# GpSimd's splits and sums in instructions of 256 columns, in a graph network with attention on one core

## The chip, the cores and the metric

The kernel runs on one core of a Trainium2 chip, in one launch. The metric is device time: the median of three runs of the kernel before is 2378.5 us (2378.1 to 2378.63). Five engines work at once and meet only at semaphores: TensorE (PE) multiplies and writes PSUM, VectorE (DVE), ScalarE (ACT) and GpSimd (POOL) do element-wise work, SyncE (SP) issues most DMAs.

## The reference

1024 nodes of 512 features in 16 graphs, 16,384 edges. All arrays are fp32.

```
h = relu(layernorm(x));  h = gcn_in(batchnorm(h))
for i in 4 layers:
    h = h + attention(ln(h), cond[16, 256, 512], Wq, Wk, Wv, Wo)   # 8 heads of 64
    u = ln(h) @ geglu_w[i] + geglu_b[i];  val, gate = split(u)      # 512 -> 4096
    h = h + (val * gelu(gate)) @ ffo_w[i] + ffo_b[i]                # 2048 -> 512
out = x + (gcn_out(h) + relu(layernorm(x)))
```

`gcn` multiplies by a weight matrix and sums over the edges with the usual degree scaling.

## The kernel before, in words

**Splits.** Every fp32 operand of a matrix product is kept as a high part (fp32r) and a low part, the rest. A product is three matmuls: high by high, high by low, low by high (lines 2367 to 2369, 2616 to 2619, 2741 to 2745). ACT writes the high parts by a copy. GpSimd or VectorE writes the low parts by a subtraction, `low = whole - high`, a TENSOR_TENSOR with two inputs in SBUF.

**Products of 2 by 2 blocks.** Keys, values and the wide MLP matrix are computed with seven block products in place of eight. That needs sums of weight blocks (`sums_s`, written by VectorE at L2250 to L2255 in the MLP and L1693 to L1698 in attention), sums of condition blocks (`cond_sum`, GpSimd, L798) and sums of activation blocks (`t_sums`, VectorE, L2227), whose low parts come from L2232 and L2237.

**Stages.** First the edges are counted and the first convolution is done (to about 180 us). Then come four layers. A layer's attention goes over 8 pairs of graphs (`value_units(t)` and `key_units(t)`, t = 0 to 7). In layer 0 only, GpSimd also makes the split blocks `cb` of the next pair's condition there, 7 low parts (`cond_low`, L803) and 4 sums a pair, and SP saves them to DRAM; later layers load them back. A layer's MLP goes over q = 0 to 7. For q = 1 to 7 there are two weight sets c = 0, 1 (`set_low(q, c)`, buffer `wg_lo`); `down_low(q)` splits the down projection (`wf_lo`), `f_low` (L864, 512 columns) the activations. The set (1, 0) is multiplied as a full block set, all others by the seven products.

**What sets the order.** Each engine runs one fixed list of instructions. Each `wait_ge` waits for a semaphore. `w_ok` counts finished low weight pieces: PE waits for it before it uses a piece (`full_product`, `set_product`, L2741), and SP before it loads the next piece into one of the two `stage` slots. `c_lo` and `c_sum` count low condition blocks and condition sums. At the start of an MLP GpSimd does, one behind the other, `down_low(0)` (L732), `set_low(1, 0)` (L890, L894), three `f_low` (L864), `set_low(1, 1)` (L890, L897). Beside it VectorE does the sums and low parts of the activations (L2227, L2232). `rsqrt` and `first_rsqrt` (L727, L773) are small powers by GpSimd, on which the layer norms wait.

Of the kernel before, what the change touches and what calls it, by code (L numbers as in the profile page):

```python
# [5 lines left out]
def gnn_preln_kernel(  # L6
# [24 lines left out]
    ALU = mybir.AluOpType  # L31
# [71 lines left out]
    with ExitStack() as ctx:  # L103
        def sb(name, shape, dt, where=ctx):
            return where.enter_context(nc.sbuf_tensor(name, shape, dt))

        def sem(name):
            return ctx.enter_context(nc.semaphore(name))


        stage = sb("stage", [P, 2, 1024], f32)
# [242 lines left out]
        c_hi, c_lo, c_sum = sem("c_hi"), sem("c_lo"), sem("c_sum")  # L354
# [8 lines left out]
        w_hi_ok, w_ok = sem("w_hi_ok"), sem("w_ok")  # L363
# [28 lines left out]
        def wait_apart(eng, on, value):  # L392


            eng.wait_ge(on, value)
            eng.sem_inc(waited, 1)

        def bits(ap):

            return ap.bitcast(f32)  # L400
# [24 lines left out]
        def attn_place(part, kind, k):  # L425
            return ((wk_hi, wk_lo), (wv_hi, wv_lo))[kind][part][:, k]
# [8 lines left out]
        def attn_piece(kind, k, l):  # L435

            if l == 0:
                return 2 + 2 * kind + k
            return FIRST_PIECES + PIECES * (l - 1) + (KEY_PIECE, VALUE_PIECE)[kind][k]
# [7 lines left out]
        def raw_block(g, n):  # L447

            row, col = {11: (0, 0), 12: (0, 1), 21: (1, 0), 22: (1, 1)}[n]
            return (stage if g else raw0)[:, row, :].rearrange("p (k b m) -> p b k m", k=2, b=2)[:, col]  # L450

        def cond_source(g, j):
            return (raw_block(g, 11), t2_s[:, :, :], t1_s[:, :, :], raw_block(g, 21), raw_block(g, 22),
                    raw_block(g, 12), raw_block(g, 11))[j]
# [30 lines left out]
        def set_piece(q, c):  # L485
            return DOWN_PIECE[q - 1] + 1 + c

        def set_place(part, c):
            return (wg_hi, wg_lo)[part][:, 1 - c].rearrange("p k v n -> p (k v n)")[:, 0:7 * 256]\
                .rearrange("p (b n) -> p b n", n=256)  # L490
# [7 lines left out]
        def short_set(l, q, c):  # L498
            return (SETS - 1) * l + 2 * (q - 1) + c - 1
# [197 lines left out]
        def _(pool):  # L697
# [31 lines left out]
            def w_low(n, slot, hi, lo):  # L729

                pool.wait_ge(w_hi_ok, n + 1)
                pool.tensor_tensor(lo, stage[:, slot, :], bits(hi), ALU.subtract).then_inc(w_ok, 1)  # L732


            pool.wait_ge(d5_ok, 1)
# [9 lines left out]
            for half in range(2):  # L745
# [8 lines left out]
                pool.tensor_scalar(x_nm[:, part], x_nm[:, part], -1.0, None, ALU.mult).then_inc(x_rs, 1)  # L754
            d_low_of(1)
            w_low(0, 0, gcn_place(0, 0), gcn_place(1, 0))
            pool.wait_ge(b_ln, 2 * KC)
            pool.tensor_scalar(x_veps[:, 0:KC], x_mv[:, 0:KC, 1], EPS, None, ALU.add).then_inc(b_rs, 1)
# [16 lines left out]
            def attn_low(kind, k, l):  # L775

                n = attn_piece(kind, k, l)
                hi, lo = attn_place(0, kind, k), attn_place(1, kind, k)
                pool.wait_ge(w_hi_ok, n + 1)
                pool.tensor_tensor(lo[:, 0:3, :], stage[:, n % 2, 256:1024].rearrange("p (b n) -> p b n", n=256),  # L780
                                   bits(hi[:, 0:3, :]), ALU.subtract)
                pool.tensor_tensor(lo[:, 3:7, :], sums_s[:, :, :], bits(hi[:, 3:7, :]), ALU.subtract)\
                    .then_inc(w_ok, 1)

            def cond_sum(g, n):

                out, a, b = ((t1_s[:, :, :], raw_block(g, 12), raw_block(g, 11)),
                             (t2_s[:, :, :], raw_block(g, 22), t1_s[:, :, :]),
                             (raw_block(g, 12), raw_block(g, 22), raw_block(g, 12)),
                             (raw_block(g, 11), raw_block(g, 21), t2_s[:, :, :]))[n]  # L790
                if n == 0:
                    wait_apart(pool, raw_in, 16 * g + 16)
                elif n == 1 or n == 2:
                    pool.wait_ge(c_sum, 4 * g + 1)
                else:
                    pool.wait_ge(c_sum, 4 * g + 2)
                    pool.wait_ge(c_lo, BLOCKS * g + 1)
                pool.tensor_tensor(out, a, b, ALU.subtract).then_inc(c_sum, 1)  # L798

            def cond_low(g, j):  # L800

                pool.wait_ge(c_hi, BLOCKS * g + j + 1)
                pool.tensor_tensor(cb[:, j, 1], cond_source(g, j), bits(cb[:, j, 0]), ALU.subtract).then_inc(c_lo, 1)  # L803

            def wq_low(l, half):

# [34 lines left out]
            first_sums()  # L841
            pool.wait_ge(a_low, NT + 1)
            attn_low(KEYS, 0, 0)
            for n in range(3):
                cond_sum(0, n)
            attn_low(KEYS, 1, 0)
            for half in range(2):
                wq_low(0, half)
            cond_low(0, 0)
            cond_sum(0, 3)  # L850
            cond_low(0, 1)
            first_rsqrt(0)
            pool.wait_ge(z2_ok, FIRST)
            for j in range(2, 5):
                cond_low(0, j)
# [3 lines left out]
            for l in range(L):  # L859
# [8 lines left out]
                def down_low(q):  # L868
                    r = DOWN_PIECE[q]
                    w_low(FIRST_PIECES + PIECES * l + r, r % 2, down_place(0, q), down_place(1, q))  # L870

                def ahead_low(q):
                    if l < L - 1:
                        attn_low(KEYS, q, l + 1)
                    else:
                        r = KEY_PIECE[q]
                        w_low(FIRST_PIECES + PIECES * l + r, r % 2, gcn_place(0, q), gcn_place(1, q))
# [4 lines left out]
                def set_low(q, c):  # L882
                    r = set_piece(q, c)
                    hi, lo = set_place(0, c), set_place(1, c)
                    full_set = (q, c) == (1, 0)
                    if not full_set:

                        pool.wait_ge(s_ok, 4 * (short_set(l, q, c) + 1))
                    pool.wait_ge(a_hi_ok, SETS * l + 2 * (q - 1) + c + 1)
                    pool.tensor_tensor(lo[:, 0:3, :], stage[:, r % 2, 256:1024].rearrange("p (b n) -> p b n", n=256),  # L890
                                       bits(hi[:, 0:3, :]), ALU.subtract)
                    pool.wait_ge(w_hi_ok, FIRST_PIECES + PIECES * l + r + 1)
                    if full_set:
                        pool.tensor_tensor(lo[:, A21, :], stage[:, r % 2, 0:256], bits(hi[:, A21, :]),  # L894
                                           ALU.subtract).then_inc(w_ok, 1)
                    else:
                        pool.tensor_tensor(lo[:, 3:7, :], sums_s[:, :, :], bits(hi[:, 3:7, :]),  # L897
                                           ALU.subtract).then_inc(w_ok, 1)

                first_rsqrt(2 * l + 1)  # L900
# [10 lines left out]
                if l == 0:  # L911
                    for n in range(3):
                        cond_sum(1, n)
# [46 lines left out]
                wait_apart(pool, x3_ok, 2 + NT * l + NT)  # L960
                down_low(0)
                set_low(1, 0)
                f_low(0, 0, 0, 0)
                f_low(0, 1, 0, 1)
                f_low(0, 2, 1, 0)
                set_low(1, 1)
                f_low(0, 3, 1, 1)
                for q in range(1, MG):
                    if q > 1:
                        down_low(q)  # L970
                    f_low(q, 0, 1, 0)
                    f_low(q, 1, 0, 0)
                    if q == 1:
                        down_low(q)
                    if q + 1 < MG:
                        set_low(q + 1, 0)
                    f_low(q, 2, 1, 1)
                    f_low(q, 3, 0, 1)
                    if q + 1 < MG:
                        set_low(q + 1, 1)  # L980
                    if q in KEYS_IN:
                        ahead_low(KEYS_IN.index(q))
# [2064 lines left out]
```

## Time and profile before

| | |
|---|---|
| median of three runs | 2378.5 us |
| the profiled execution | 2377.68 us |
| its span | 2375.9 us |
| granted TensorE clock, mean | 0.996 |
| PE busy | 2315.6 us, 97% |
| VectorE busy | 1658.8 us, 70% |
| ScalarE busy | 1243.8 us, 52% |
| GpSimd busy | 1038.9 us, 44% |

PE, the bound, has 60.3 us without work in the span. Times of the rows are microseconds from the span's start. An idle time in brackets is what the engine waited before the row, with the instruction that ended it. An instruction's duration counts from its start to its end, and holds what it waited for a port.

### The profile page before, as it was taken

The page shows a single profiled execution, that of the slowest core. Times are in us where ns is not written, and L with a number is a line of the kernel's source. Part 1 is how long each engine was busy: PE and PEld are TensorE (multiplying, and loading weights), DVE is VectorE, ACT ScalarE, POOL GpSimd, SP SyncE. Part 2 cuts the span into 40 slices and gives each one's busy share as a digit, 9 for nine tenths or more (in the row PEclk, how much of TensorE's full clock was granted, in tenths as well). Part 3 has the DMA queues.
Part 4 walks back from the last instruction along what each step waited for, and adds up shares of the span by engine and source line. Part 5 has one row for each costly group of instructions (what it writes and reads, how often), then busy time and mean ns, then how long its engine had stood idle before and what let it go on. Part 6 is the DMA issues. An engine that isn't in the chain of part 4 may idle for free.

```text
span 2375.9 us, 38716 instructions
## 1 busy us (share of the span) xinstructions
PE 2315.6 (97%) x14414; PEld 2043.8 (86%) x14414; DVE 1658.8 (70%) x3053; ACT 1243.8 (52%) x2585; POOL 1038.9 (44%) x696
## 2 busy tenths in 40 slices
PE   7899999999999999999999999999999999999999
PEld 5358999988888999988888999988888999988887
DVE  9976776786657676786657666786667667785554
ACT  9955767654434555653434555644434655643322
POOL 3025877566653322266652322266652322265530
PEclk9999999999999999999999999999999999999999
DMA  2033333212232333212232333222232433122230
GB/s 80 1 132 135 146 148 152 98 49 67 62 120 79 118 106 106 82 54 62 63 120 80 123 107 106 74 60 61 61 117 81 125 116 108 63 63 62 62 125 36
DMA packets 115882, 214.57 MB, mean 90 GB/s; under 512 B 9520, under 2 KB 71600, under 8 KB 113904
## 3 DMA queue, kind: packets, MB, share of 16 engines
q1 hardware_dynamic: 115408, 207.89, 26.6%
q10 hardware_dynamic: 288, 4.19, 0.4%
q8 instruction: 117, 1.92, 0.3%
q14 instruction: 69, 0.57, 0.1%
HBM read 176.13 MB, written 35.91 MB: 89 GB/s over the span
## 4 chain that ended last, share of the span: by engine, by line
PE 84%; DVE 9%; POOL 2%; ACT 2%; issue 2%; DMA 0%; DVEq 0%; SPq 0%; ACTq 0%; POOLq 0%
PE ps L2367 9%; PE ps L2368 9%; PE ps L2369 9%; PE ps L2616 9%; PE ps L2619 8%; PE ps L2618 8%; PE ps L2741 7%; PE ps L2743 7%; PE ps L2745 7%; PE ps L2644 2%; PE ps L2666 2%; PE ps L2668 2%; DVE oh_d L1683 1%; PE ps L2943 1%; PE ps L2663 1%
## 5 line engine op out<-in xcount | busy, mean ns | idle before, releaser
L2616 PE MATMUL ps<-cb,wk_hi 128*128 128x256 f32 x896 | 258.3, 288 | 4.6 <-POOL cb L803 3.6
L2616 PE MATMUL ps<-wv_hi,cb 128*128 128x256 f32 x896 | 257.4, 287 | 4.6 <-DVE kv L1985 4.4
L2618 PE MATMUL ps<-cb,wk_hi 128*128 128x256 f32 x896 | 253.7, 283 | 0.0
L2619 PE MATMUL ps<-cb,wk_lo 128*128 128x256 f32 x896 | 253.7, 283 | 0.0
L2619 PE MATMUL ps<-wv_hi,cb 128*128 128x256 f32 x896 | 253.7, 283 | 0.0
L2618 PE MATMUL ps<-wv_lo,cb 128*128 128x256 f32 x896 | 253.7, 283 | 0.0
L864 POOL TENSOR_TENSOR f_lo<-ff,f_hi 128x512 fp32r<-128x512 f32 x128 | 168.7, 1329 | 172.0 <-ACT f_hi L1484 171.9
L823 POOL TENSOR_TENSOR v_lo<-kv,v_hi 128x512 fp32r<-128x512 f32 x96 | 124.4, 1296 | 260.2 <-ACT v_hi L1238 260.1
L2302 DVE TENSOR_TENSOR h<-h,ps 128x512 f32<-128x512 f32 x256 | 169.3, 684 | 65.4 <-PE ps L2369 64.8
L2368 PE MATMUL ps<-wf_lo,f_hi 128*128 128x512 f32 x512 | 199.3, 389 | 0.0
L2367 PE MATMUL ps<-wf_hi,f_hi 128*128 128x512 f32 x512 | 199.3, 389 | 0.0
L2369 PE MATMUL ps<-wf_hi,f_lo 128*128 128x512 f32 x512 | 199.3, 389 | 0.0
L2741 PE MATMUL ps<-xT_hi,wg_hi 128*128 128x512 f32 x480 | 187.8, 391 | 11.2 <-POOL wg_lo L897 6.8
L2743 PE MATMUL ps<-xT_lo,wg_hi 128*128 128x512 f32 x480 | 187.0, 390 | 0.0
L2745 PE MATMUL ps<-xT_hi,wg_lo 128*128 128x512 f32 x480 | 186.9, 389 | 0.0
L1985 DVE TENSOR_TENSOR kv<-ps,kv 128x512 f32<-128x512 f32 x192 | 132.3, 690 | 70.8 <-PE ps L2619 66.4
L2616 PEld LDWEIGHTS ps<-cb,wk_hi 128*128 128x128 f32 x896 | 171.7, 192 | 10.9 <-POOL cb L803 5.0
L2616 PEld LDWEIGHTS ps<-wv_hi,cb 128*128 128x128 f32 x896 | 171.7, 192 | 7.8 <-DVE kv L1985 5.8
L2618 PEld LDWEIGHTS ps<-cb,wk_hi 128*128 128x128 f32 x896 | 171.9, 192 | 1.1
L2618 PEld LDWEIGHTS ps<-wv_lo,cb 128*128 128x128 f32 x896 | 171.9, 192 | 0.0
L2619 PEld LDWEIGHTS ps<-wv_hi,cb 128*128 128x128 f32 x896 | 171.9, 192 | 0.0
L2619 PEld LDWEIGHTS ps<-cb,wk_lo 128*128 128x128 f32 x896 | 171.8, 192 | 0.0
(377 smaller groups left out, 6892.0 us busy)
## 6 DMA issues: line engine op xcount, KB each, us to landing
cb<-cb_s SPq DMA_DIRECT2D x168, 512.0 KB, 4.6
stage<-in_pieces SPq DMA_DIRECT2D x256, 128.0 KB, 2.6
cb_s<-cb SPq DMA_DIRECT2D x56, 512.0 KB, 2.6
stage<-in_pieces SPq DMA_DIRECT2D x44, 512.0 KB, 3.7
stage<-in_condT SPq DMA_DIRECT2D x7, 1024.0 KB, 5.8
stage<-in_pieces SPq DMA_DIRECT2D x16, 256.0 KB, 3.3
at_s<-at_hi ACTq DMA_DIRECT2D x2, 2048.0 KB, 11.8
wo_raw<-in_pieces SPq DMA_DIRECT2D x8, 512.0 KB, 4.4
```

Of the source, the lines that this page charges most:

```text
L864: pool.tensor_tensor(f_lo[q % 2][:, c, half * HALF:(half + 1) * HALF], ff[:, s % 2, :], bits(f_hi[q % 2][:, c, half * HALF:(half + 1) * HA ...
L1985: dve.tensor_tensor(wide(kv_temp(which)), ps[:, bank, :], wide(other[:, :, :]), ALU.add)\
L2302: dve.tensor_tensor(h[:, t, :], h[:, t, :], ps[:, down_bank(q, t), :], ALU.add)\
L2367: pe.matmul(bank, l_hi, r_hi, start=(first and i == 0), stop=False)
L2368: pe.matmul(bank, l_hi, r_lo, start=False, stop=False)
L2369: end = pe.matmul(bank, l_lo, r_hi, start=False, stop=(last and i == n - 1))
L2616: pe.matmul(to, l_hi, r_hi, start=(fresh and i == 0 and k == 0), stop=False, skip_group_check=True)
L2618: pe.matmul(to, l_hi, r_lo, start=False, stop=False, skip_group_check=True)
L2619: last = pe.matmul(to, l_lo, r_hi, start=False, stop=(k == 1), skip_group_check=True)
L2741: pe.matmul(ps[:, bank, :], hi[:, a, r], moving[0][:, n, :], start=(first and n == 0), stop=False, skip_group_check=True)
L2743: pe.matmul(ps[:, bank, :], hi[:, a, r], moving[1][:, n, :], start=False, stop=False, skip_group_check=True)
L2745: last = pe.matmul(ps[:, bank, :], lo[:, a, r], moving[0][:, n, :], start=False, stop=(n == 1), skip_group_check=True)
```

## The change

Four places of GpSimd's program are cut into instructions of 256 columns: `w_low` (1024 columns), `attn_low` (768 and 1024), `cond_sum` and `cond_low` (512), and `set_low` (768 and 1024). The semaphore is raised by the last piece alone. `f_low`, `kv_low`, `wq_low` and `wo_low` stay as they are, and so do all other engines.

```diff
             def w_low(n, slot, hi, lo):
                 pool.wait_ge(w_hi_ok, n + 1)
-                pool.tensor_tensor(lo, stage[:, slot, :], bits(hi), ALU.subtract).then_inc(w_ok, 1)
+                for c in range(0, 768, 256):
+                    pool.tensor_tensor(lo[:, c:c + 256], stage[:, slot, c:c + 256], bits(hi[:, c:c + 256]), ALU.subtract)
+                pool.tensor_tensor(lo[:, 768:1024], stage[:, slot, 768:1024], bits(hi[:, 768:1024]), ALU.subtract)\
+                    .then_inc(w_ok, 1)
...
             # attn_low; set_low has the same two loops
-                pool.tensor_tensor(lo[:, 0:3, :], stage[:, n % 2, 256:1024].rearrange("p (b n) -> p b n", n=256),
-                                   bits(hi[:, 0:3, :]), ALU.subtract)
-                pool.tensor_tensor(lo[:, 3:7, :], sums_s[:, :, :], bits(hi[:, 3:7, :]), ALU.subtract)\
-                    .then_inc(w_ok, 1)
+                for b in range(3):
+                    pool.tensor_tensor(lo[:, b, :], stage[:, n % 2, 256 * b + 256:256 * b + 512], bits(hi[:, b, :]),
+                                       ALU.subtract)
+                for b in range(3):
+                    pool.tensor_tensor(lo[:, 3 + b, :], sums_s[:, b, :], bits(hi[:, 3 + b, :]), ALU.subtract)
+                pool.tensor_tensor(lo[:, 6, :], sums_s[:, 3, :], bits(hi[:, 6, :]), ALU.subtract).then_inc(w_ok, 1)
...
             # cond_sum
-                pool.tensor_tensor(out, a, b, ALU.subtract).then_inc(c_sum, 1)
+                pool.tensor_tensor(out[:, 0], a[:, 0], b[:, 0], ALU.subtract)
+                pool.tensor_tensor(out[:, 1], a[:, 1], b[:, 1], ALU.subtract).then_inc(c_sum, 1)
             def cond_low(g, j):
                 pool.wait_ge(c_hi, BLOCKS * g + j + 1)
-                pool.tensor_tensor(cb[:, j, 1], cond_source(g, j), bits(cb[:, j, 0]), ALU.subtract).then_inc(c_lo, 1)
+                hi, lo, source = bits(cb[:, j, 0]), cb[:, j, 1], cond_source(g, j)
+                pool.tensor_tensor(lo[:, 0], source[:, 0], hi[:, 0], ALU.subtract)
+                pool.tensor_tensor(lo[:, 1], source[:, 1], hi[:, 1], ALU.subtract).then_inc(c_lo, 1)
```

GpSimd at the start of a layer's MLP, before (`wf_lo` and `wg_lo` are low weights, `f_lo` low activations):

```order
L732 TENSOR_TENSOR wf_lo<-stage,wf_hi 128x1024
L890 TENSOR_TENSOR wg_lo<-stage,wg_hi 128x768
L894 TENSOR_TENSOR wg_lo<-stage,wg_hi 128x256
L864 TENSOR_TENSOR f_lo<-ff,f_hi 128x512 x3
L890 TENSOR_TENSOR wg_lo<-stage,wg_hi 128x768
L897 TENSOR_TENSOR wg_lo<-sums_s,wg_hi 128x1024
L864 TENSOR_TENSOR f_lo<-ff,f_hi 128x512 x3
```

and in the changed kernel:

```order
L733 TENSOR_TENSOR wf_lo<-stage,wf_hi 128x256 x3
L734 TENSOR_TENSOR wf_lo<-stage,wf_hi 128x256
L899 TENSOR_TENSOR wg_lo<-stage,wg_hi 128x256 x3
L903 TENSOR_TENSOR wg_lo<-stage,wg_hi 128x256
L872 TENSOR_TENSOR f_lo<-ff,f_hi 128x512 x3
L899 TENSOR_TENSOR wg_lo<-stage,wg_hi 128x256 x3
L907 TENSOR_TENSOR wg_lo<-sums_s,wg_hi 128x256 x3
L908 TENSOR_TENSOR wg_lo<-sums_s,wg_hi 128x256
L872 TENSOR_TENSOR f_lo<-ff,f_hi 128x512 x3
```

Nothing changes places: ahead of the first `f_lo` there are eight instructions in place of three. VectorE's list beside it is the same in both kernels (`z` are the activations and their sums, `w_lo` here their low parts):

```order
L2232 TENSOR_TENSOR w_lo<-z,w_hi 128x3x2x128
L2227 TENSOR_TENSOR z<-z 128x3x256 x2
L2227 TENSOR_TENSOR z<-z 128x256 x4
L2232 TENSOR_TENSOR w_lo<-z,w_hi 128x3x2x128 x2
L2217 SCALAR_TENSOR_TENSOR ff<-ps,cols_sb,gel 128x512
L2250 TENSOR_TENSOR sums_s<-stage 128x256
```

All but the one with `ps` have two inputs in SBUF.

## Rows read from the trace of the kernel before

**Rows 1.** The page's first part: busy us (share of the span), instructions.

```profile
PE 2315.6 (97%) x14414; PEld 2043.8 (86%) x14414; DVE 1658.8 (70%) x3053; ACT 1243.8 (52%) x2585; POOL 1038.9 (44%) x696
```

**Rows 2.** PE's waits over the whole span: us in total, times, longest us.

```profile
PE ps L2741 <- POOL wg_lo L897: 6.8, 4, 1.7
PE ps L2741 <- POOL wg_lo L894: 4.4, 4, 1.1
PE ps L2616 <- POOL cb L803: 3.6, 7, 0.7
```

**Rows 3.** A group by form on GpSimd: busy us, mean ns, idle before.

```profile
L897 POOL TENSOR_TENSOR wg_lo<-sums_s,wg_hi 128x1024 fp32r<-128x1024 f32 x52 | 125.5, 2414 | 0.0
```

**Rows 4.** Timeline of GpSimd, 96 to 99 us: start us, us, instruction.

```profile
96.57 0.72 POOL L831 TENSOR_TENSOR sums_s<-stage 128x256 f32<-128x256 f32 x1 [58.06 <-DVE counts L1807]
97.26 0.72 POOL L832 TENSOR_TENSOR sums_s<-stage 128x256 f32<-128x256 f32 x1
```

**Rows 5.** Timeline of GpSimd, 166 to 181 us.

```profile
166.71 1.86 POOL L780 TENSOR_TENSOR wk_lo<-stage,wk_hi 128x768 fp32r<-128x768 f32 x1 [5.23 <-ACT wk_hi L1015]
168.52 2.39 POOL L782 TENSOR_TENSOR wk_lo<-sums_s,wk_hi 128x1024 fp32r<-128x1024 f32 x1
...
178.31 1.29 POOL L803 TENSOR_TENSOR cb<-t_s,cb 128x512 fp32r<-128x512 f32 x1
179.56 1.01 POOL L773 TENSOR_TENSOR x_veps<-x_veps,mhalf 128x4 f32<-128x4 f32 x1
```

**Rows 6.** Timeline of VectorE, 27 and 252 us.

```profile
27.50 0.16 DVE L1669 TENSOR_TENSOR bn<-x_veps,cols_sb 128x4 f32<-128x4 f32 x1 [0.69 <-POOL x_veps L760]
...
252.75 2.80 DVE L2018 TENSOR_TENSOR qbd<-z,qbd 64x256 fp32r<-64x256 f32 x2
```

**Rows 7.** Timeline of PE in layer 0, the instructions that waited.

```profile
182.58 0.33 PE L2684 MATMUL ps<-ident,o_full 128*128 128x128 f32 x1 [1.23 <-DVE p_exp L1937]
...
227.57 0.39 PE L2616 MATMUL ps<-wv_hi,cb 128*128 128x256 f32 x1 [1.07 <-DVE kv L1985]
...
238.99 0.38 PE L2616 MATMUL ps<-cb,wk_hi 128*128 128x256 f32 x1 [0.68 <-POOL cb L803]
...
258.78 0.39 PE L2616 MATMUL ps<-wv_hi,cb 128*128 128x256 f32 x1 [1.01 <-DVE kv L1985]
```

**Rows 8.** Timeline of ScalarE, 234 us.

```profile
234.75 0.60 ACT L1219 ACTIVATE kv<-ps 128x512 f32<-128x512 f32 x1 [2.54 <-POOL v_lo L823]
```

**Rows 9.** Timeline of GpSimd at the start of layer 0's MLP, and later in it.

```profile
488.63 2.99 POOL L732 TENSOR_TENSOR wf_lo<-stage,wf_hi 128x1024 fp32r<-128x1024 f32 x1 [5.03 <-DVE xT_lo L2091]
491.58 2.58 POOL L890 TENSOR_TENSOR wg_lo<-stage,wg_hi 128x768 fp32r<-128x768 f32 x1
494.12 1.43 POOL L894 TENSOR_TENSOR wg_lo<-stage,wg_hi 128x256 fp32r<-128x256 f32 x1
...
504.09 1.86 POOL L890 TENSOR_TENSOR wg_lo<-stage,wg_hi 128x768 fp32r<-128x768 f32 x1 [0.36 <-DVE sums_s L2255]
505.91 2.54 POOL L897 TENSOR_TENSOR wg_lo<-sums_s,wg_hi 128x1024 fp32r<-128x1024 f32 x1
...
608.45 2.41 POOL L897 TENSOR_TENSOR wg_lo<-sums_s,wg_hi 128x1024 fp32r<-128x1024 f32 x1
```

**Rows 10.** Timeline of VectorE there; the last row from a wide window merges six.

```profile
488.38 0.96 DVE L2232 TENSOR_TENSOR w_lo<-z,w_hi 128x768 fp32r<-128x768 f32 x1
489.26 3.18 DVE L2227 TENSOR_TENSOR z<-z 128x768 f32<-128x768 f32 x1
...
489.26 9.91 DVE L2227 TENSOR_TENSOR z<-z 128x768 f32<-128x768 f32 x6
```

**Rows 11.** Timeline of PE there, and at a later set (619 us).

```profile
495.61 0.50 PE L2741 MATMUL ps<-xT_hi,wg_hi 128*128 128x512 f32 x1 [1.10 <-POOL wg_lo L894]
508.51 0.50 PE L2741 MATMUL ps<-xT_hi,wg_hi 128*128 128x512 f32 x1 [1.72 <-POOL wg_lo L897]
...
619.15 0.39 PE L2741 MATMUL ps<-xT_hi,wg_hi 128*128 128x512 f32 x1
```

More of the change, by code:

```diff
@@ L889, in set_low @@
                     pool.wait_ge(a_hi_ok, SETS * l + 2 * (q - 1) + c + 1)
-                    pool.tensor_tensor(lo[:, 0:3, :], stage[:, r % 2, 256:1024].rearrange("p (b n) -> p b n", n=256),
-                                       bits(hi[:, 0:3, :]), ALU.subtract)
+                    for b in range(3):
+                        pool.tensor_tensor(lo[:, b, :], stage[:, r % 2, 256 * b + 256:256 * b + 512],
+                                           bits(hi[:, b, :]), ALU.subtract)
                     pool.wait_ge(w_hi_ok, FIRST_PIECES + PIECES * l + r + 1)
@@ L896, in set_low @@
                     else:
-                        pool.tensor_tensor(lo[:, 3:7, :], sums_s[:, :, :], bits(hi[:, 3:7, :]),
+                        for b in range(3):
+                            pool.tensor_tensor(lo[:, 3 + b, :], sums_s[:, b, :], bits(hi[:, 3 + b, :]), ALU.subtract)
+                        pool.tensor_tensor(lo[:, 6, :], sums_s[:, 3, :], bits(hi[:, 6, :]),
                                            ALU.subtract).then_inc(w_ok, 1)
```

## The prediction

> **What bounds the kernel now.** I read the page's busy shares first. PE works 2315.6 us of the 2375.9 us span [rows 1], so the time can move only by its 60.3 us of idle time, or by new idle time. Next come PE's waits. Few name GpSimd: 6.8 us for the last piece of the set (1, 1), 4.4 us for that of the set (1, 0), once each a layer, and 3.6 us for condition blocks in layer 0 [rows 2]. So GpSimd's 1038.9 us are mostly hidden, and the question is where its later end shows. I then read the timelines around each of these waits.
>
> **What one cut costs.** GpSimd's 256-column subtractions of the trace last 0.72 us and follow each other at 97.26 - 96.57 = 0.69 us [rows 4]. The 768-column one is followed after 168.52 - 166.71 = 1.81 us, the 512-column one after 179.56 - 178.31 = 1.25 us [rows 5], the 1024-column one lasts 2.39 to 2.41 us [rows 3, 5], a pitch of about 2.37. Cut up: 3 x 0.69 = 2.07, 2 x 0.69 = 1.38, 4 x 0.69 = 2.76. So one more instruction costs about 0.13 us: +0.26 for 768, +0.13 for 512, +0.39 for 1024 columns.
> By the code there are 43 `w_low` (3 more instructions each), 15 `attn_low` (5 more), 56 `set_low` (2 more) of which 52 have sums (3 more), 56 `cond_low` and 32 `cond_sum` (1 more): 129 + 75 + 268 + 88 = 560 more instructions, 560 x 0.13 = 73 us of GpSimd's time.
> The Trainium skill, GPSIMD Engine Reference, section Elementwise — side-by-side cycle accounting, gives 4497 ns for 2048 columns and 2.6 cycles a column at 1.2 GHz, which leaves an estimated 60 ns for what an instruction costs beside its columns. By that, 560 cuts would be 34 us; the rows of this trace say twice as much, and they decide.
>
> **What a cut changes for VectorE.** The timelines at 488 to 496 us show the two engines taking turns at one port. VectorE's L2227 of 768 columns lasts 3.18 us while GpSimd's L732 runs, and ends 0.8 us behind it; an uncontended one of that size lasts 0.96 us (the L2232 at 488.38) [rows 9, 10]. GpSimd's next, L890, lasts 2.58 us where 1.86 is normal, its L894 1.43 us where 0.72 is [rows 4, 9]. So each instruction with two SBUF inputs waits for one of the other engine: 0.72 us if VectorE's has 768 columns. From the ends of these rows, a turn takes 0.60 us for 256 columns on GpSimd, and 0.80 us (768) or 0.27 us (256) on VectorE. Pieces shorten VectorE's waits, and give it more turns between GpSimd's.
> The Trainium skill, SBUF — State Buffer, section Who interferes with whom, says that the second to issue waits until the first has finished. It does not say who is served next when GpSimd has more in its queue; on that see rival A.
>
> **Term 1, the MLP's start, four times.** Before, GpSimd did L732, L890 and L894 from 488.63 and PE began the full set at 495.61, after 1.10 us of idle time [rows 9, 11]. Now there are 4 + 3 + 1 = 8 pieces. VectorE has queued, in its order, the L2232 under way, L2227 with 768, 768, 256, 256, 256, 256 columns, and L2232 with 768. With one turn each, from 489.25 (when the L2232 leaves the port): 8 x 0.60 + 3 x 0.80 + 4 x 0.27 = 8.28, to 497.53; with 0.1 for the end, PE begins at 497.65, 2.04 us later.
> In return VectorE has its sums of activations 4 us sooner. But its next `ff` (L2217) waits for a `f_low` of GpSimd, which now comes later, and its weight sums take turns with two more `f_low`, about 1.17 us each (1.25 less the gap). By the same turns the last sum (L2255) ends at 503.2, where it ended at 504.02. GpSimd then has 3 + 4 pieces, 7 x 0.60 = 4.20, between which VectorE takes three turns of 256 columns and one of 1024 (0.27 x 3 + 1.07), then two gaps of 0.09: from 503.3 to about 509.55. PE needs 508.51 - 1.72 - 495.61 = 11.18 us for the full set, so is ready at 508.83, and starts the next set at 509.65 in place of 508.51. **+1.1 us a layer, +4.4 us**. Bounds: if the second set is in time, PE's own shift stays, 508.83 - 508.51 = +0.3; if VectorE takes more turns in the second stretch too, +2.0; and if the earlier sums win outright, -1.1 (rival C). What is queued behind the cut instructions on GpSimd (`f_low`) is needed by the down projection only after the next set.
>
> **Term 2, layer 0's first attention steps.** From 166.71 GpSimd works without a gap to 180.57; PE's transposes wait 1.23 us for a layer norm that waits for L773 [rows 5, 7]. Ahead of it now are one `attn_low` (+0.26 + 0.39) and three condition instructions (+0.39). **+1.0 us**; bounds 0.6 (if PE has slack that the rows do not show) and 1.3.
>
> **Term 3, the second pair's condition blocks.** The `attn_low` of the values (+0.65, of which the shorter turns of VectorE's `qbd` give back some) releases the load of the next condition, and two `cond_sum` (+0.26) the copy behind which the wait of 1.07 us at 227.57 stands: +0.85. Six more condition instructions stand ahead of ScalarE's copy at 234.75, which waited 2.54 us for GpSimd [rows 8], and one in PE's wait at 238.99 [rows 7]: together +0.65 + 9 x 0.12, +1.7. At 252.75 VectorE's two `qbd` take 2.80 us beside 512-column sums, where two turns of 0.6 and their own 0.85 make 1.85 [rows 6]: 0.95 back. With three more cuts ahead (+0.36) the wait at 258.78 ends +1.1 later than before, and that is what stays, since PE arrives there 1.7 - 1.01 = 0.7 later. **+1.1 us**; bounds 0.3 and 2.3.
>
> **Term 4, the other pairs.** Six times PE waits 0.49 us ((3.6 - 0.68) / 6) for a `cond_low` that starts after a small power [rows 2, 7]: 6 x 0.12, **+0.7 us**; bounds 0 and 1.
>
> **Term 5, the start.** `w_low(0)` stands ahead of the batch norm's power, and VectorE waits 0.69 us for it [rows 6]; VectorE sets the pace there. **+0.4 us**; bounds 0 and 0.5.
>
> **At nothing.** In the MLP's other sets GpSimd's last piece ended at 608.45 + 2.41 = 610.86, PE took up that set at 619.15 [rows 9, 11]: 8.3 us of cover for about 1.3 us of cuts a set and its neighbours. Without cover it would cost 0.65 us at each of 48 sets, 31 us. Loads that start later, by up to 2 us, are hidden the same way.
>
> **Sum.** 4.4 + 1.0 + 1.1 + 0.7 + 0.4 = 7.6 us. On the profiled execution, 2377.68 + 7.6 = 2385.3; that execution stands 0.8 us under the median, so the median is to be 2386.1: **2386 us**, slower by 0.32%.
>
> **Rivals.**
> A, GpSimd keeps the port through its own queue. Then the eight pieces run from 489.25 in 8 x 0.69 = 5.5 us, PE begins 0.7 us sooner, VectorE falls behind, and the second set ends at about 509.0: +0.5 a layer. 3.2 + 2.0 = 5.2, so 2383.7. Against it: between L732, L890 and L894, which stood ready in the queue, VectorE did get a turn each time [rows 9, 10].
> B, the cuts are hidden. If the pieces overlap so that 256 columns cost no more than a quarter of 1024 (0.59), terms 2 to 5 vanish and term 1 keeps some turns: 0 to +3 us, about 2379.5. For it: PE's idle time is only 2.5% [rows 1]. Against it: the pitch of 0.69 is measured on four such instructions [rows 4].
> C, the other side: VectorE's relief decides. Place: the second wait at the MLP's start, 1.72 us. If the weight sums end over 1.5 us sooner than in my turns (before 501.7), the second set is ready before PE is; if also the first wait grows only by 5 cuts, 0.65 us, a layer gains 1.72 - 0.65 = 1.07, 4.3 in all. It decides once terms 2 to 5 come to less than 4.3; at their lower bounds (0.9) the time is 2375.1. For it: VectorE's six L2227 take 9.91 us [rows 10], of which at 0.96 us for 768 and 0.42 us for 256 columns 2 x 0.96 + 4 x 0.42 = 3.6 us are work. Against it: the `ff` that waits for `f_low`.
> D, the turns hurt more: +2.0 in term 1 and the upper bounds elsewhere: 8.0 + 5.1 = 13.1, so 2391.6.
>
> **How the numbers follow.** My forecast (the sum within 2.5 us) 0.45, A 0.13, B 0.21, C 0.08, D 0.13. About 0.2%, 4.8 us, is what can be told from no change: the bound is 2383.3. My forecast and D lie above it but for 0.03 of the forecast, A by half: slower 0.62. Within it are 0.03 of the forecast, half of A, 0.20 of B and 0.03 of C, whose 2375.1 is itself too near: same 0.32. Faster by over 0.2% is the rest of C, where both waits go, and 0.01 of B: 0.06. The range leaves out C's lower end and D's upper: 2378 to 2391.
>
> **What would show it.** GpSimd's busy time 60 to 90 us higher, 1256 instructions. VectorE's six L2227 at the MLP's start within 6 to 7 us. PE's wait for the full set about 3.1 us, for the next about 0.8. PE's wait before the transposes 2.2 us, for condition blocks some 0.6 each. My account is wrong if the wait for the full set stays below 2 us, if PE waits for GpSimd at sets of q over 1, or if the time falls.

## The result and the profile after

The changed kernel takes 2387.8 us (median of 6 runs, 2387.1 to 2389.1), the kernel before, on the same chip, 2378.3 (2377.1 to 2378.6): 1.0042 times as long, 95% interval 1.0032 to 1.0053, so 9.5 us slower. The forecast was 2386, slower, in a range of 2378 to 2391. The profiled execution has a span of 2386.0 us, 10.1 more than before.

The first part of the page after (busy us, share of the span, instructions):

```profile
PE 2318.6 (97%) x14414; PEld 2048.2 (86%) x14414; DVE 1645.2 (69%) x3053; ACT 1244.8 (52%) x2585; POOL 1131.0 (47%) x1256
```

Against [rows 1], GpSimd is 92.1 us busier with 560 more instructions, 0.16 us each: by the rows 0.13 is the instruction's own, and the rest I put down to waits at the port. VectorE is 13.6 us less busy. Neither number is the loss; that stands in PE's waits (us in total, times, longest):

```profile
PE ps L2752 <- POOL wg_lo L903: 12.9, 4, 3.2
PE ps L2627 <- POOL cb L811: 6.1, 8, 1.3
PE ps L2752 <- POOL wg_lo L908: 1.1, 1, 1.1
```

They answer to [rows 2]: the wait for the full set rose from 4.4 to 12.9 us, that for the second set fell from 6.8 to 1.1, that for condition blocks rose from 3.6 to 6.1.

To see where the time went, I compared the moments at which PE goes on after its last wait ahead of each layer's MLP. Its timeline before, then after (start us, us, instruction, idle time before it):

```profile
488.50 0.38 PE L2367 MATMUL ps<-xT_hi,w_hi 128*128 128x256 f32 x1 [0.43 <-DVE xT_lo L2091]
...
1021.24 0.38 PE L2367 MATMUL ps<-xT_hi,w_hi 128*128 128x256 f32 x1 [0.43 <-DVE xT_lo L2091]
...
1553.77 0.38 PE L2367 MATMUL ps<-xT_hi,w_hi 128*128 128x256 f32 x1 [0.43 <-DVE xT_lo L2091]
...
2086.25 0.38 PE L2367 MATMUL ps<-xT_hi,w_hi 128*128 128x256 f32 x1 [0.43 <-DVE xT_lo L2091]
```

```profile
492.08 0.39 PE L2378 MATMUL ps<-xT_hi,w_hi 128*128 128x256 f32 x1 [0.43 <-DVE xT_lo L2102]
...
1026.18 0.38 PE L2378 MATMUL ps<-xT_hi,w_hi 128*128 128x256 f32 x1 [0.43 <-DVE xT_lo L2102]
...
1559.84 0.39 PE L2378 MATMUL ps<-xT_hi,w_hi 128*128 128x256 f32 x1 [0.43 <-DVE xT_lo L2102]
...
2093.75 0.39 PE L2378 MATMUL ps<-xT_hi,w_hi 128*128 128x256 f32 x1 [0.43 <-DVE xT_lo L2102]
```

Ahead of the first MLP 492.08 - 488.50 = 3.58 us were lost. From each of these moments to the next, or to the end (289.65 us before, 292.25 after), 1.36, 1.13, 1.43 and 2.60 were lost, 6.5 us in all. The run `mlp_start_only` below places them at the MLP's start.

Layer 0's start on GpSimd, then VectorE, then PE:

```profile
492.20 4.15 POOL L733 TENSOR_TENSOR wf_lo<-stage,wf_hi 128x256 fp32r<-128x256 f32 x3 [5.04 <-DVE xT_lo L2102]
496.32 0.92 POOL L734 TENSOR_TENSOR wf_lo<-stage,wf_hi 128x256 fp32r<-128x256 f32 x1
497.21 2.66 POOL L899 TENSOR_TENSOR wg_lo<-stage,wg_hi 128x256 fp32r<-128x256 f32 x3
499.83 1.44 POOL L903 TENSOR_TENSOR wg_lo<-stage,wg_hi 128x256 fp32r<-128x256 f32 x1
```

```profile
492.83 6.45 DVE L2238 TENSOR_TENSOR z<-z 128x768 f32<-128x768 f32 x6
...
506.56 0.43 DVE L2266 TENSOR_TENSOR sums_s<-stage,sums_s 128x256 f32<-128x256 f32 x1
```

```profile
501.32 0.70 PE L2752 MATMUL ps<-xT_hi,wg_hi 128*128 128x512 f32 x1 [3.22 <-POOL wg_lo L903]
501.82 0.63 PE L2754 MATMUL ps<-xT_lo,wg_hi 128*128 128x512 f32 x1
502.24 0.63 PE L2756 MATMUL ps<-xT_hi,wg_lo 128*128 128x512 f32 x1
...
505.31 0.40 PE L2754 MATMUL ps<-xT_lo,wg_hi 128*128 128x512 f32 x1
505.54 0.40 PE L2756 MATMUL ps<-xT_hi,wg_lo 128*128 128x512 f32 x1
...
1047.68 0.50 PE L2752 MATMUL ps<-xT_hi,wg_hi 128*128 128x512 f32 x1 [1.10 <-POOL wg_lo L908]
```

VectorE's six sums take 6.45 us where they took 9.91 [rows 10]; GpSimd's eight pieces take 9.1 where three took 6.9 [rows 9]; PE waits 3.22 us, and in layer 1 alone 1.10 more for the second set. This is the turn-taking of the forecast. What the matmuls show next is not in the forecast: one of 512 columns follows the one before after 0.43 us at first (501.82, 502.24), after 0.23 later (505.31, 505.54). The windows there (length, busy us and instructions of PE, PEld, DVE, ACT and POOL, PE's granted clock, DMA share, GB/s):

```profile
498.00:501.00 3.00, 0.10 (x1) 0.00 (x0) 2.96 (x4) 0.99 (x2) 3.00 (x4) 1.00 0.52 142
501.00:504.00 3.00, 2.68 (x7) 2.11 (x8) 1.83 (x3) 0.00 (x0) 3.00 (x3) 0.58 0.47 168
504.00:507.00 3.00, 3.00 (x13) 2.41 (x12) 2.96 (x6) 1.95 (x3) 1.95 (x2) 0.86 0.10 40
507.00:510.00 3.00, 3.00 (x15) 2.49 (x14) 3.00 (x5) 2.98 (x4) 2.94 (x4) 1.00 0.00 0
1035.00:1038.00 3.00, 2.59 (x11) 2.18 (x12) 1.81 (x2) 0.00 (x0) 3.00 (x3) 1.00 0.64 188
```

After PE's idle 3.2 us the clock fell to its lower level, 1.2 GHz, for 3 to 4 us in the layers 0 and 2 and for about twice as long in layer 3. It did not fall in layer 1 (the last row), with the same wait. The forecast has nothing on this.

### The profile page after: what moved, and what is told of

Same layout as the page of the kernel before. It is cut to its first block, busy times and chain, and to the rows that moved or that the text cites. A ratio compares the mean times of both kernels' runs of the same rounds, so it can differ in the third digit from the quotient of the medians.

```text
span 2386.0 us, 39276 instructions
## 1 busy us (share of the span) xinstructions
PE 2318.6 (97%) x14414; PEld 2048.2 (86%) x14414; DVE 1645.2 (69%) x3053; ACT 1244.8 (52%) x2585; POOL 1131.0 (47%) x1256
## 4 chain that ended last, share of the span: by engine, by line
PE 85%; DVE 7%; POOL 5%; ACT 2%; issue 1%; DMA 0%; SPq 0%; DVEq 0%; ACTq 0%; POOLq 0%
PE ps L2378 9%; PE ps L2379 9%; PE ps L2380 9%; PE ps L2627 9%; PE ps L2630 8%; PE ps L2629 8%; PE ps L2752 8%; PE ps L2754 7%; PE ps L2756 7%; PE ps L2655 2%; PE ps L2677 2%; PE ps L2679 2%; DVE oh_d L1694 1%; PE ps L2954 1%; PE ps L2674 1%; DVE oh_d L1812 1%
## 5 line engine op out<-in xcount | busy, mean ns | idle before, releaser
L2752 PE MATMUL ps<-xT_hi,wg_hi 128*128 128x512 f32 x480 | 190.1, 396 | 14.0 <-POOL wg_lo L903 12.9
L831 POOL TENSOR_TENSOR kT_lo<-kv,kT_hi 128x512 fp32r<-128x512 f32 x96 | 123.8, 1292 | 108.7 <-ACT kT_hi L1249 79.4
```

The source lines that it names most:

```text
L831: pool.tensor_tensor(kv_place(1, kind, *KV_LATER[n]), kv_temp(n), bits(kv_place(0, kind, *KV_LATER[n])), ALU.subtract).then_inc(kv_ok, 1)
L2752: pe.matmul(ps[:, bank, :], hi[:, a, r], moving[0][:, n, :], start=(first and n == 0), stop=False, skip_group_check=True)
```

## The experiments

Each was timed in five rounds beside the kernel before, on one chip a group; the kernel before took 2377.8, 2377.7 and 2377.9 us in the three groups. There are twelve kernels; none leaves out or changes part of the computation.

**Where the loss stands.** Four kernels cut one part of the instructions each. The edit is the change's own, made for these alone; together they are all 560 instructions.

`mlp_start_only`: at `down_low` and `set_low`,

```diff
-                    w_low(FIRST_PIECES + PIECES * l + r, r % 2, down_place(0, q), down_place(1, q))
+                    w_low(FIRST_PIECES + PIECES * l + r, r % 2, down_place(0, q), down_place(1, q), cut=q == 0)
...
+                    if q == 1:
```

> The kernel before, with only the pieces at the MLP's start cut (the first down weights, both sets of q = 1, in each of the four layers); all else whole. My theory (one turn each at the shared port, and a clock that falls after the longer wait): the profile after grew by 6.5 us in the four MLP starts, so this one gives +5.5 to +7 us over the kernel before, with waits of about 3.2 us for the full set in each layer. The forecast's own term 1 said +4.4. Rival B (cuts hidden): 0 to +3. Rival A (GpSimd keeps the port): +2.

Measured: 2384.3 us (8 runs, 2383.1 to 2385.5), +6.5; 1.0028 (1.0017 to 1.0038). The four waits for the full set sum to 12.9 us again. Rivals A (+2) and B (at most +3) fall.

`late_sets_only`: the same with `cut=q > 0` and `if q > 1:`, 324 of the 560 added instructions.

> The kernel before, with only the MLP's later pieces cut (the down weights of q over 0 and the sets of q over 1): by far most of the added instructions. My theory: 0 us within 0.5, since 8.3 us of cover stand ahead of PE at each set, while GpSimd's busy time rises by some 50 us. Rival: every cut costs something where it stands (loads later, VectorE's turns), which would give +2 us or more.

Measured: 2377.6 us, -0.2; 1.0000 (0.9990 to 1.0009). GpSimd's busy time rose by 47.8 us, 0.148 an instruction:

```profile
PE 2315.6 (97%) x14414; PEld 2043.6 (86%) x14414; DVE 1674.5 (70%) x3053; ACT 1245.2 (52%) x2585; POOL 1086.7 (46%) x1020
```

More than half of the change is free: its work has 8 us of cover. VectorE's busy time rose too, by 15.7 us, and no wait of PE grew with it.

`cond_attn_only`: `attn_low`, `cond_sum` and `cond_low` as in the change, nothing else.

> The kernel before, with only the splits of the attention's weights and the condition's sums and splits cut. My theory: terms 2 to 4, which the profile after puts at about +3.3 us in layer 0, and nothing in the later layers (the splits of attention weights stand there beside the MLP, where GpSimd has slack). The forecast's own terms gave +2.8. Rival B (hidden): 0 to +1. Rival D: +4.7 and more.

Measured: 2381.6 us, +3.7; 1.0016 (1.0007 to 1.0025). My theory's 3.3 holds within the scatter; B falls.

`rest_only`: the whole-piece splits outside the down weights.

```diff
-            def w_low(n, slot, hi, lo):
+            def w_low(n, slot, hi, lo, cut=True):
...
-                    w_low(FIRST_PIECES + PIECES * l + r, r % 2, down_place(0, q), down_place(1, q))
+                    w_low(FIRST_PIECES + PIECES * l + r, r % 2, down_place(0, q), down_place(1, q), cut=False)
```

> The kernel before with only the whole-piece splits outside the down weights cut (those of the graph convolution and the up projection's first weights): what the forecast's term 5 speaks of, +0.4 us by the split ahead of the batch norm. The start of the graph convolution's last product moved by only 0.2 us in the profile after and by 0.4 us between runs where nothing ahead of it was changed, so I now expect 0, within 0.5 us. Rival (each cut costs where it stands): +1 us or more.

Measured: 2378.2 us, +0.2; 1.0002 (0.9993 to 1.0011). The four parts sum to 6.5 - 0.2 + 3.7 + 0.2 = 10.2 us, the whole is 9.5: they add up within the scatter of the runs.

**What the MLP's start loses, and to what.** `second_only` cuts the set (1, 1) alone, `if (q, c) == (1, 1):` in `set_low`; `first_only` cuts `down_low(0)` and the set (1, 0), with `cut=q == 0` and `if (q, c) == (1, 0):`.

> The kernel before, with only the set (1, 1) cut: 2 pieces become 7, behind the weight sums, in each of the four layers. By my turns the last piece ends 6.3 us after the last sum where it took 4.4: PE's second wait is 3.6 us in place of 1.7, +1.9 us a layer, +7.7 us, and up to 2 us a layer more if the clock falls after it. Rival (a cut costs 0.13 us and no turn): 5 x 0.13 = 0.65 us a layer, +2.6 us.

Measured: 2390.9 us (2388.4 to 2392.0), +13.2; 1.0054 (1.0040 to 1.0068). The page's wait, and the windows around it in layer 0:

```profile
PE ps L2755 <- POOL wg_lo L901: 14.9, 4, 3.8
```

```profile
507.00:510.00 3.00, 0.00 (x0) 0.00 (x0) 1.77 (x2) 0.27 (x1) 3.00 (x4) 1.00 0.00 0
510.00:513.00 3.00, 2.89 (x10) 2.28 (x11) 1.35 (x2) 0.98 (x2) 1.30 (x2) 0.75 0.32 94
513.00:516.00 3.00, 3.00 (x11) 2.42 (x10) 0.69 (x1) 2.45 (x4) 2.79 (x3) 0.68 0.28 81
```

The waits sum to 14.9 us where they summed to 6.8 [rows 2]: +2.0 a layer, by turns 1.9, and not 0.65. The clock fell after all four of them, and a layer lost 3.3 us in all, so 1.3 went to the clock. This one small cut is dearer than the whole change. There the first cuts let VectorE's last weight sum end 0.6 us sooner and PE begin the full set 2.1 us later, so that of the second wait 1.1 us are left where the clock stays up, and nothing where it falls.

> The kernel before, with only the first down weights and the full set (1, 0) cut: the eight pieces ahead of PE's first wait, in each of the four layers. By my turns the wait for the full set is 3.2 us again, and the second set (1, 1) is then in time (about 507.6 in layer 0, where PE is ready at 508.8), so the second wait is gone. If the granted clock stays at 1.00 that is +0.3 us a layer, +1.2 us in all. If it falls after the wait of 3.2 us, as in the changed kernel, the full set takes 1.3 to 2.6 us longer in about three layers and nothing swallows it: +4 to +8 us. Rival (a cut costs 0.13 us and no turn): the first wait grows by 0.65 us, and the second shrinks by as much: 0.

Measured: 2381.4 us (11 runs, 2376.6 to 2385.7), +3.8; 1.0016 (1.0007 to 1.0025). That is just under the range of the theory, and the scatter is six times that of the kernel before. In the profiled run the clock stayed at 1.00 in layers 0 and 1 and fell in 2 and 3:

```profile
1562.00:1565.00 3.00, 1.99 (x5) 1.60 (x6) 1.83 (x3) 0.00 (x0) 3.00 (x3) 0.50 0.53 133
1565.00:1568.00 3.00, 3.00 (x9) 2.32 (x8) 3.00 (x4) 1.94 (x3) 2.63 (x2) 0.50 0.27 111
```

Layers with the clock up took 0.2 to 0.3 us less than before, those with it down 2.4 and 1.2 us more.

**Is it the idle time that lowers the clock?** `after_filled` and `first_filled` add to the changed kernel and to `first_only`, ahead of the wait in `full_product`:

```diff
+                    for _ in range(13):
+                        pe.matmul(ps[:, z, :], up_first(0)[:, 0, 0, 0:P], xT3_hi[0][:, 0, :], start=True, stop=True,
+                                  skip_group_check=True)
```

> The changed kernel, with 13 more matmuls of 512 columns on PE ahead of its wait for the full set (about 3.05 us at 0.235 us each), into a bank that the full set overwrites. They end before the set is there, so they delay nothing. My theory: the granted clock falls at the full set because PE stood idle for 3.2 us. With PE busy the clock stays at 1.00, the full set takes 11.2 us again in layers 0, 2 and 3, and the kernel is 1 to 2.5 us faster than the changed one (2385.5 to 2387), with a second wait of some 1.1 us in every layer. Rival: the clock's fall comes from something else (the load of the power supply after the set begins, or chance): it falls here too, and the time is that of the changed kernel, 2387.8, or above if the added work keeps the clock down.

> The kernel before with the first down weights and the full set cut, and PE filled with 13 more matmuls ahead of its wait for the full set, as in the filled version of the changed kernel. Without the fill this edit gave +3.8 us, in runs from 2376.6 to 2385.7. My theory: +0.3 us a layer of waiting, and the rest and the scatter are the clock. So here +1.2 us (2378.9), all runs within 2 us of each other, and the second wait at 0 to 0.3 us. Rival (the rest is a true wait): +3.8 again.

Measured: `after_filled` 2386.3 us (2385.7 to 2387.1), +8.4; 1.0035 (1.0022 to 1.0049). `first_filled` 2377.3 us (2375.9 to 2378.3), -0.7; 0.9997 (0.9987 to 1.0006), against +3.8 without the fill. The timeline of `after_filled` at the full set, and one window each of `first_filled` in layers 2 and 3:

```profile
498.87 3.14 PE L2774 MATMUL ps<-xT_hi,w_hi 128*128 128x512 f32 x13
502.29 0.50 PE L2752 MATMUL ps<-xT_hi,wg_hi 128*128 128x512 f32 x1 [0.29 <-POOL wg_lo L903]
```

```profile
1562.00:1565.00 3.00, 2.71 (x13) 2.06 (x12) 1.81 (x2) 0.00 (x0) 3.00 (x3) 1.00 0.74 181
...
2094.00:2097.00 3.00, 2.71 (x12) 1.92 (x11) 1.81 (x3) 0.00 (x0) 3.00 (x3) 1.00 0.61 148
```

Work that computes nothing kept the clock up in all eight starts, and the scatter of `first_only` went (9 us to 2.5). `first_only` became faster beyond the intervals; in the changed kernel the gain is 1.1 us by the medians, and there the intervals overlap. The rival, that something else than PE's idle time lowers the clock, falls. From the layers' lengths in `after_filled` a start costs 1.28, 1.26, 1.23 and 1.12 us with the clock up: 4.9. The other 1.6 of the 6.5 us in the profile after are the clock's, and 1.5 of them stand in layer 3: in the layers 0 and 2 the slower full set took little more than the second wait that it hid. I had expected +1.2 us of `first_filled` and it was -0.7, with layers of 532.53, 532.31, 532.32 and 289.44 us, 0.2 us under those of before. The removed second wait is worth more than its 1.72 us: before, PE's matmuls at 508.51 [rows 11] and just behind it start 2.11, 0.34, 0.43 and 0.34 us after the one ahead of them, and 0.23 elsewhere, which is 2.30 us in all. The last two, 0.3 us of it, are a short stall for VectorE's low parts of the sums, which ended at 510.17.

**Earlier instead of smaller.** GpSimd stands idle for 5.03 us ahead of these pieces [rows 9], since one wait ahead of all of them is for the last token tile's split.

```diff
-                wait_apart(pool, x3_ok, 2 + NT * l + NT)
+                wait_apart(pool, x3_ok, 2 + NT * l + NT - 1)
```

`before_early` is this alone, `early_cut` this with the cuts of `first_only`, `after_early` this in the changed kernel.

> The kernel before (nothing cut), with one number changed: GpSimd starts the MLP's first pieces once the last but one token tile is split (483.2 us in layer 0) in place of the last (488.6). Both of PE's waits for GpSimd (1.1 and 1.7 us a layer, 11.3 us in all) go. But its pieces of 768 and 1024 columns now hold the port while VectorE makes the sums ahead of the last tile's split, for which PE waits: by turns the split ends about 1.7 us later, 7 us in four layers. So -4 us, 2374. Rival (no harm at the port): -11, 2367. Other rival (the first pieces are no bound): 0.

> The same earlier start, with the first down weights and the full set (1, 0) cut into pieces of 256 columns: VectorE then waits at most 0.6 us for a turn. The last tile's split ends 0.3 us later on average, 1.2 us in four layers, so -10 us, 2368, and the cut is then worth some 6 us against the uncut one. Rival (turns don't matter): the same time as the uncut one with the earlier start.

> The changed kernel (everything cut) with the earlier start of the MLP's first pieces. The run with the earlier start and only the first set cut has PE wait 0.88 us for the last split and 0.32 us for the second set, per layer. With the second set cut too, that one ends 1.9 us later: PE waits 2.2 us there. Against the kernel before a layer then changes by -1.1 - 1.7 + 2.2 + 0.45 = -0.2 us, -0.6 in all, and the condition and attention cuts bring +3.7: +3 us, 2380.7, if the clock stays at 1.00 after 2.2 us of idle time; up to 4 us more if it falls. Rival (the cut of the second set costs 0.65 us): 2375.

Measured: `before_early` 2372.7 us, -4.9; 0.9979 (0.9970 to 0.9988). `early_cut` 2370.2 us, -7.5; 0.9968 (0.9956 to 0.9980). `after_early` 2382.0 us (2380.5 to 2384.2), +4.0; 1.0018 (1.0009 to 1.0028). VectorE's timeline in `before_early`, then in `early_cut`:

```profile
483.86 2.64 DVE L2078 TENSOR_SCALAR z<-h,mv,rstd 128x512 f32<-128x512 f32 x1 [0.44 <-POOL rstd L727]
...
487.08 3.35 DVE L2227 TENSOR_TENSOR z<-z 128x768 f32<-128x768 f32 x2
490.36 0.68 DVE L2091 TENSOR_TENSOR xT_lo<-z,xT_hi 128x512 fp32r<-128x512 f32 x1
```

```profile
483.65 0.96 DVE L2098 TENSOR_SCALAR z<-h,mv,rstd 128x512 f32<-128x512 f32 x1 [0.44 <-POOL rstd L727]
...
485.20 2.94 DVE L2247 TENSOR_TENSOR z<-z 128x768 f32<-128x768 f32 x2
488.06 1.23 DVE L2111 TENSOR_TENSOR xT_lo<-z,xT_hi 128x512 fp32r<-128x512 f32 x1
```

Both of PE's waits (11.3 us together) went, and behind GpSimd's 1024 columns VectorE's normalization, 0.55 us of work, took 2.64; PE waits 1.6 us for it in each layer. With pieces of 256 columns it takes 0.96. So here the cut is worth 2.6 us, of the 6 that I expected: the place of the stall was another (the normalization, not the split's own turn), and its size smaller. PE's timeline of `before_early` and the windows behind that wait in layer 0:

```profile
486.56 0.66 PE L2717 MATMUL ps<-ident,z 128*128 128x128 f32 x4 [1.57 <-DVE z L2078]
```

```profile
486.00:489.00 3.00, 2.44 (x15) 2.20 (x16) 3.00 (x4) 1.63 (x5) 3.00 (x3) 0.84 0.30 88
489.00:492.00 3.00, 3.00 (x18) 3.00 (x18) 3.00 (x4) 2.50 (x4) 1.78 (x2) 0.59 0.72 199
```

Here the clock fell after only 1.6 us of idle time, in the layers 0 and 3 and not in 1 and 2. Counted from the last product ahead of that wait, the layers 0 to 3 took 0.87, 1.33, 1.34 and 0.99 us less than before, and 1.9 to 2.0 each in `early_cut`, where the clock stayed up. So by this estimate some 0.8 of the 3.2 us by which these two profiled runs differ are the clock's. `early_cut` missed its 2368 by 2.2: PE waits 0.88 for the split where it waited 0.43, 0.3 at the second set, and 7.5 remain of 11.3. The rival, that turns don't matter, falls. In `after_early` the cut second set makes PE wait 2.3 us; the clock fell after one of these four waits. Counted in the same way, the three other layers took 0.2 to 0.3 us less than before, where I had expected 0.2, and the one with the fall took 1.3 more. Its +4.0 lies in the range that its expectation gave for a falling clock.

`early_cut_cond5` adds, in `key_units`:

```diff
+                    if l == 0 and not last:
+                        cond_low(g, 5)
                     if t and not last:
                         rsqrt(GROUPS * l + t - 1)
                     if l == 0 and not last:
-                        cond_low(g, 5)
                         cond_low(g, 6)
```

> The earlier start with the first set cut, and in layer 0 the split of condition block 5 put ahead of the layer norm's small power on GpSimd, for the six pairs where PE waits 0.49 us for it. My theory: 6 x 0.49 = 2.9 us less than without that move (2370.2), so 2367.3. Rival: the power, 0.6 us later, is what PE waits for next (through VectorE), and nothing is gained: 2370.

Measured: 2368.2 us (2367.9 to 2368.6), -9.7; 0.9960 (0.9946 to 0.9974). Against `early_cut` it is 1.9 us (2.2 with each against its own runs of before), of 2.9 expected: the waits for the condition blocks are gone from the head of the list, and those for VectorE's `kv` rose from 5.5 to 7.1 us, so the rival had a part.

```profile
PE ps L2637 <- DVE kv L2006: 7.1, 14, 1.0
```

This is the fastest version: it beats the kernel before by 9.7 us and the changed one by some 19.

## Why the prediction was right

The direction and the mechanism were right, the time 1.8 us too low. The range, 2378 to 2391, held no change as well, so the time alone would not have told the turns from hidden cuts; the waits and `mlp_start_only` do. By its steps:

**The price of a cut** (0.13 us) held. GpSimd's timeline after, where layer 0's attention begins:

```profile
166.89 2.14 POOL L784 TENSOR_TENSOR wk_lo<-stage,wk_hi 128x256 fp32r<-128x256 f32 x3 [3.62 <-ACT wk_hi L1026]
168.98 2.12 POOL L787 TENSOR_TENSOR wk_lo<-sums_s,wk_hi 128x256 fp32r<-128x256 f32 x3
```

Three pieces take 168.98 - 166.89 = 2.09 us from start to start, 3 x 0.69 and a little, where 768 columns in one took 1.81 [rows 5]. GpSimd's busy time grew by 92 us, just above the 60 to 90 that I had named as a sign.

**Term 1**, +4.4, measured 6.5. Counted from PE's row at 488.50 or 492.08, the full set begins 9.24 us later (forecast 9.15), the last weight sum ends after 14.9 (forecast 14.7), the second set, where the clock stayed up, begins after 1047.68 - 1026.18 = 21.50 (forecast 21.15). The turns are right to 0.35 us at every step. The term is mis-sized by the clock, 1.6 us, which no step has, and by 0.1 a layer in the rest. The forecast's second wait, 0.8, was 1.1, and shows only where the clock stayed up; where it fell, the slower full set hid that wait. "The earlier sums win" (C) fell: VectorE did finish its six sums 3.5 us sooner, and its next `ff` then waited for the `f_low`, 1.17 us, as said.

**Term 2**, +1.0: the transposes stand at 183.86 where they stood at 182.58, of which 0.21 was there already at the last product of the graph convolution (at 140.28, before at 140.07): +1.07. But the sign that I named was wrong: the wait at the transposes stayed at 1.23 us, and the delay shows as a new wait ahead of it, at 180.93. PE's timeline after:

```profile
180.93 0.39 PE L2627 MATMUL ps<-cb,wk_hi 128*128 128x256 f32 x1 [0.92 <-POOL cb L811]
183.86 0.33 PE L2695 MATMUL ps<-ident,o_full 128*128 128x128 f32 x1 [1.23 <-DVE p_exp L1948]
229.92 0.39 PE L2627 MATMUL ps<-wv_hi,cb 128*128 128x256 f32 x1 [2.14 <-DVE kv L1996]
...
242.21 0.39 PE L2627 MATMUL ps<-cb,wk_hi 128*128 128x256 f32 x1 [0.82 <-POOL cb L811]
...
277.25 0.39 PE L2627 MATMUL ps<-cb,wk_hi 128*128 128x256 f32 x1 [1.25 <-POOL cb L811]
```

**Term 3**, +1.1, measured 1.84. At 242.21 PE is 3.22 us behind, 1.94 more than at the transposes (forecast 1.7). The wait at 258.78 [rows 7] went, and VectorE's `qbd` takes 1.29 where it took 2.80 [rows 6], as said. (My working has it at 1.85, but its own terms, two turns of 0.6 and 0.85, make 2.05.) But what I took for a gain of 0.6 was none: the third pair's block at 277.25 waits 1.25 us where it waited 0.48, and PE is still 3.12 behind. The step that failed is that the loss ends at 258.78. ScalarE's copy waited for GpSimd there as it did at 234.75 [rows 8], a pair later, and longer than before (2.67 us at 266.19). ScalarE's timeline after:

```profile
269.57 0.60 ACT L1230 ACTIVATE kv<-ps 128x512 f32<-128x512 f32 x1 [3.73 <-POOL v_lo L831]
```

**Term 4**, +0.7: from 3.12 behind to 3.58 at the MLP, +0.46. The waits of 0.49 became 0.62, so the 0.12 a block is right; of the six blocks that I counted, the first lies at 274.13 and so in term 3's stretch, and 5 x 0.12 = 0.6 remain, of which 0.46 are seen.

**Term 5**, +0.4: VectorE waits 0.94 us for the batch norm's power where it waited 0.69 [rows 6], but nothing of it is seen at the product that follows, beyond the 0.2 by which runs differ there. Sum of terms 2 to 5: 3.2 forecast, 3.6 measured with those 0.2; `cond_attn_only` (terms 2 to 4) gave 3.7, `rest_only` (term 5) 0.2.

**At nothing**: right, -0.2 us for 324 cuts.

So of the 1.8 us that the forecast is low, the clock is 1.6 by the layers' lengths of the two profiled runs, and 9.5 - 8.4 = 1.1 by the medians of the changed kernel and of `after_filled`, each against its own runs of before. The rest of term 1 and the second place of term 3 make up the remainder, less what terms 4 and 5 were too high. That the forecast came so near is in part luck: its terms were low by 2.9 us in terms 1 to 3 and high by 0.4 in the others, and what the clock adds differs from run to run.

## What to carry to other kernels

Where two engines with full queues take turns at one port, count turns and not columns: cutting one engine's instructions relieves the other and costs itself a turn of the other for each added piece. So cut where the partner's short work is on the critical path (here -2.6 us beside an earlier start, the clock's part in it included), not where the cut engine's own result is waited for (+2.0 us a layer). Look first at why the awaited work starts so late: moving one wait by one tile was worth 4.9 us, more than any size of piece alone. And where a change lengthens an idle stretch of TensorE, the granted clock behind it is to be read too: in `second_only` it added 1.3 us to each 2.0 us of waiting.

## What the runs showed of the hardware

**TensorE's clock after a short idle stretch.** In the profiled runs it fell to 1.2 GHz after four of four waits of 3.7 us (`second_only`), after eight of twelve of 3.2 us (the changed kernel, `mlp_start_only`, `first_only`), after one of four of 2.3 us (`after_early`), after two of four of 1.6 us (`before_early`), and after none of the 1.1 and 1.7 us of the kernel before, nor in the eight filled starts. So the length of the wait alone does not tell: a wait of 1.6 us was followed by a fall, and one of 3.2 us was not. A fall cost 1.3 to 2.6 us where no later wait hid it. What decides stays open. The fill with matmuls that compute nothing kept the clock up each time. The Trainium skill, TensorE: Matmul & The Clock Gate, Part 1: The HAM clock gate, says that the gate looks at PE's recent activity at times of its own, which do not start with the kernel. By that rule equal waits may end differently, as they did; no run here shows those times.

**The two engines at the port.** So these two engines do not meet at semaphores alone, as the kernel's description has it. VectorE's `TENSOR_SCALAR` with one input tensor was held up by GpSimd's subtraction as the two-input sums are (2.64 us in place of 0.55); I had counted only the latter. VectorE's `ff`, with a PSUM input, kept its 0.74 to 0.75 us in all these timelines. The Trainium skill, SBUF — State Buffer, section Who interferes with whom, has one of the two wait for the other, and the runs agree; that they then take turns, one instruction each, is what `second_only` (+2.0 us for five more pieces) shows beyond it.
